# Splitting the mix of a soft mixture-of-experts layer into fp32r products of high and low parts

## The chip, the cores and the metric

The kernel runs on one core of a Trainium2 chip. The time is the device time of one execution in microseconds (us). Before the change it is 192.72 us, the median of three runs (192.67 to 193.3).

## The reference

One perceiver layer on x (128 rows of 256), all in fp32:

```python
x = x + cross_attention(layernorm(x), ctx)      # ctx: 12544 rows of 256
x = x + hyena(layernorm(x))                     # two long convolutions, gated
x = x + soft_moe(layernorm(x))

# soft_moe, E = 16 experts with 64 slots each, F = 512
x  = layernorm(x, norm_g, norm_b)
se = layernorm(slot_embeds, slot_g, slot_b) * scale
logits   = einsum('bnd,esd->bnes', x, se)
dispatch = softmax(logits, axis=1)
combine  = softmax(logits.reshape(b, n, E * S), axis=-1)
slots = einsum('bnd,bnes->besd', x, dispatch)
gate  = gelu(einsum('besd,edf->besf', slots, Wg) + bg)
up    = einsum('besd,edf->besf', slots, Wu) + bu
eout  = einsum('besf,efo->beso', gate * up, Wd) + bd
return einsum('bns,bso->bno', combine, eout)    # the mix
```

## The kernel before

The program is written by hand: each engine has its own list of instructions, in the order in which they run, and semaphores tie the lists together. Three stages follow one another. The attention (to 104 us of the span) goes over 98 tiles of 128 context rows in groups of four. It already works with split operands: a tile is kept as a high part, rounded to fp32r, and a low part, the remainder, and a product of two such operands is three fp32r matmuls (high by high, high by low, low by high). For the context rows POOL makes half of the high parts (L1001, a sum with a zero that is broadcast) and all low parts (L1006, a difference); PE weighs them at L457, L459 and L461. The hyena stage follows, to 124 us.

The last stage is the layer of experts, from 125 us on. Sixteen experts are taken as eight pairs p of 128 slots. For each pair PE computes gate and up (`hidden_of`, L663: per expert a 64-column weight tile and 512 moving columns, fp32), transposes the product of the two (`hidden_transpose`, L718), multiplies by the down weights into bank 4 (`down_of`, L676) and adds the pair's share of the output (`mix_of`, L726). DVE adds the bias to gate (L1276) and up (L1288), multiplies them into hid (L1297) and adds the down bias into eout (L1319), which has two buffers. ACT computes the gelu (L947), copies the transposed hid (L975) and issues the load of the bias rows for the pair three later (L977 to L980). There are three slots of bias rows, and DVE waits for a slot before the gate of its pair (L1270). SP has issued all weight loads by 153.2 us. In this stage POOL has no work.

The order on PE is the loop at L738. In turn p it issues gate of pair p, the transposes of pair p-1, a mix, up of pair p, and down of pair p-1. The mixes stand so: pairs 0 and 1 in turn 3, pair 2 in turn 4, pair 3 in turn 5, pair 4 in turn 6, none in turn 7. In turn 8, which has no gate and no up, pair 5 comes ahead of the last transposes, pair 6 behind them, and pair 7 after the last down, in two halves. A mix of the kernel before is two fp32 matmuls with combT[p] as weights and 128 columns of eout as the moving side, one into bank 1 and one into bank 5, accumulated over all eight pairs. In the profile each fp32 matmul is two records.

combT, the transposed combine weights, is written by ACT in turn 2 (`combine_copy`, L939) into the tile that held the transposed dispatch weights. The pieces of the tail: ACT and DVE copy half of the last transposed hid each (L972, L1307), DVE adds the bias to the two halves of the last eout (L1312), and after the last mixes DVE scales by rs and adds x2 (L1327). Two output DMAs follow.

Of the kernel before, what the change touches and what calls it, by code (L numbers as in the profile page):

```python
# [13 lines left out]
def perceiver_kernel(nc, x, ctx_in, xattn_W, proj_w, proj_b, filter_time, norm_g, norm_b,  # L14
                     scale, slot_embeds, Wg, Wu, Wd, biases, columns, tables, out):
    fp32 = mybir.dt.float32
    fp32r = mybir.dt.float32r
    ALU = mybir.AluOpType
# [3 lines left out]
    P = 128  # L22
    D = x.shape[2]
    DK = D // P
# [27 lines left out]
    with st:  # L52
        def sem(name):
            return st.enter_context(nc.semaphore(name))

        def sb(name, shape, dt=fp32, where=st):
            return where.enter_context(nc.sbuf_tensor(name, shape, dt))
# [3 lines left out]

        tab = sb("tab", [P, 5, P])
        ident, dft_c, dft_s, inv_c, inv_s = (tab[:, i, :] for i in range(5))
        x_sb = sb("x_sb", [P, D])
        x1 = sb("x1", [P, D])
        x2 = sb("x2", [P, D])
        xh = sb("xh", [P, D])
        xhT = sb("xhT", [P, DK, P])
        xn = sb("xn", [P, D])
        xnT = sb("xnT", [P, DK, P])  # L70
        stat6 = sb("stat6", [P, 6])
        mv = sb("mv", [P, 2])
        rstd = sb("rstd", [P, 1])
# [60 lines left out]
        ffn = ExitStack()  # L134
        late_gu = [sb(f"late_gu{i}", [P, 2, 2, DK, F], fp32, ffn) for i in range(EARLY, WSLOTS - 1)] + [last_gu]
        late_d = [sb(f"late_d{i}", [P, 2, FC, D], fp32, ffn) for i in range(EARLY, WSLOTS - 1)] + [last_d]
        dT = sb("dT", [P, PAIRS, P], fp32, ffn)
        combT = dT
        disp = sb("disp", [P, P], fp32, ffn)
        disp_hi = sb("disp_hi", [P, 4 * P], fp32r, ffn)  # L140
        disp_lo = sb("disp_lo", [P, 4 * P], fp32r, ffn)
        xn_hi = sb("xn_hi", [P, D], fp32r, ffn)
        xn_lo = sb("xn_lo", [P, D], fp32r, ffn)
        comb = sb("comb", [P, SLOTS], fp32, ffn)
        cmax = sb("cmax", [P, PAIRS], fp32, ffn)
        csum = sb("csum", [P, PAIRS], fp32, ffn)
        cinv = sb("cinv", [P, PAIRS], fp32, ffn)
# [58 lines left out]
        slots_ps, slots_rdy = sem("slots_ps"), sem("slots_rdy")  # L206
        rmax_rdy, cexp_rdy = sem("rmax_rdy"), sem("cexp_rdy")
        combT_ps, combT_rdy = sem("combT_ps"), sem("combT_rdy")
        gate_ps, up_ps, gate_rdy, up_rdy = sem("gate_ps"), sem("up_ps"), sem("gate_rdy"), sem("up_rdy")
        gelu_rdy, hid_rdy, hidT_ps, hidT_rdy = (sem("gelu_rdy"), sem("hid_rdy"), sem("hidT_ps"),  # L210
                                                sem("hidT_rdy"))
# [63 lines left out]
        def cols(h):  # L275
            return slice(h * P, (h + 1) * P)
# [90 lines left out]
        UP_BANK = (2, 0)  # L367
        SE_BANK = (6, 4, 2, 6)
        V_BANK, FREQ_BANK, CONV_BANK = (2, 0), (4, 1), (5, 3)
        MIX_BANK = (1, 5)  # L370

        LAST_T_BANK, LAST_DOWN_BANK = (3, 0), (4, 6)

# [2 lines left out]
        def _(pe):  # L376
# [347 lines left out]
                last.then_inc(hidT_ps, 1)  # L724

            def mix_of(p):  # L726
                pe.wait_ge(eout_rdy, p + 1)
                if p == 0:
                    pe.wait_ge(combT_rdy, 2)
                for h in range(2):  # L730
                    if p == PAIRS - 1:
                        pe.wait_ge(eout_rdy, p + 1 + h)
                    last = nc.tensor.matmul(bank[MIX_BANK[h]][:, 0:P], combT[:, p, :], eout[:, p % 2, cols(h)],  # L733
                                            start=(p == 0), stop=(p == PAIRS - 1))
                    if h == 1 or p == PAIRS - 1:
                        last.then_inc(mix_ps, 1)

            for p in range(PAIRS + 1):  # L738
                if p < PAIRS:
                    if p in (0, 1, 3):  # L740

                        pe.wait_ge(slots_rdy, {0: 2, 1: 4, 3: 6}[p])
                    if p >= 2:
                        pe.wait_ge(gate_rdy, p - 1)
                    hidden_of(p, 0, (6, 7)[p % 2], gate_ps)
                if p == 0:
                    logits(2)
                    first_logits_back()
                    transpose_dispatch(1)

                if p == PAIRS:
                    mix_of(PAIRS - 3)
                if p == PAIRS:
                    last_transpose()
                elif p >= 2:
                    hidden_transpose(p - 1)
                if p == 3:
                    mix_of(0)
                if p >= 3 and p != PAIRS - 1:
                    mix_of(p - 2)  # L760
                if p < PAIRS:
                    if p >= 2:
                        pe.wait_ge(up_rdy, p - 1)
                    hidden_of(p, 1, UP_BANK[p % 2], up_ps)
                if p == 0:
                    gather(1)
                    transpose_logits(2)
                    hidden_transpose(0)
                if p == 2:
                    transpose_dispatch(2)  # L770
                    combine_transpose(0)
                if p == PAIRS:
                    last_down()
                elif p >= 1:
                    down_of(p - 1)
                if p == 2:
                    gather(2)
                    combine_transpose(1)
# [204 lines left out]
        @block.gpsimd  # L983
        def _(pool):
            nc.gpsimd.memset(zero[:, :], 0.0).then_inc(const_set, 1)
            nc.gpsimd.memset(neg_half[:, :], -0.5).then_inc(const_set, 1)
            nc.gpsimd.memset(ones_sq[:, :], 1.0).then_inc(sq_set, 1)
            pool.wait_ge(const_set, 2)

            def power(n, dst, src, width):  # L990
                pool.wait_ge(var_rdy, n + 1)
                nc.gpsimd.tensor_tensor(dst, src, neg_half[:, 0:width], ALU.pow).then_inc(rstd_rdy, 1)

            power(0, rstd[:, 0:1], mv[:, 1:2], 1)

            def split_ctx(loop, g, slot, nt):

                pool.wait_ge(ld_raw[slot], raw_count(loop, g))
                if loop is not None or g >= RING:
                    pool.wait_ge(pv_ps, times(loop, g - RING + 1))  # L1000
                nc.gpsimd.tensor_tensor(c_hi[:, slot, 0:nt // 2, 0:D], raw[:, slot, 0:nt // 2, :],  # L1001
                                        zero[:, 0:1].unsqueeze(2).broadcast_to([P, nt // 2, D]), ALU.add
                                        ).then_inc(chi_rdy, 1)
                pool.wait_ge(chi_rdy, times(loop, g + 1))
                pool.wait_ge(chi2_rdy, times(loop, g + 1))
                nc.gpsimd.tensor_tensor(c_lo[:, slot, 0:nt, :], raw[:, slot, 0:nt, :],  # L1006
                                        c_hi[:, slot, 0:nt, 0:D].bitcast(fp32), ALU.subtract
                                        ).then_inc(clo_rdy, 1)

            for g in range(RING):  # L1010
                split_ctx(None, g, g, GT)
            with pool.Fori(0, LOOPS) as n:
                for u in range(RING):
                    split_ctx(n, RING + u, u, GT)
            split_ctx(None, LAST, LAST % RING, LAST_T)
            power(1, rstd[:, 0:1], mv[:, 1:2], 1)
            power(2, se_rstd[:, :], se_mv[:, :, 1], PAIRS)
            power(3, rstd[:, 0:1], mv[:, 1:2], 1)


        @block.vector
        def _(dve):
            count = [0]

            def link(ins):

                count[0] += 1
                ins.then_inc(dve_n, 1)
                dve.wait_ge(dve_n, count[0])
# [238 lines left out]
            for p in range(PAIRS + 1):  # L1268
# [36 lines left out]
                if p == PAIRS:  # L1305
                    dve.wait_ge(hidT_ps, p + 1)
                    nc.vector.tensor_copy(hidT[:, 2:4, :].rearrange("p c s -> p (c s)"),  # L1307
                                          bank[LAST_T_BANK[1]][:, 0:2 * P]).then_inc(hidT2_rdy, 1)
                    dve.wait_ge(mix_ps, p - 2)
                    for h in range(2):  # L1310
                        dve.wait_ge(down_ps, p + h)
                        nc.vector.tensor_tensor(eout[:, (p - 1) % 2, cols(h)], bank[LAST_DOWN_BANK[h]][:, 0:P],  # L1312
                                                bias[:, (p - 1) % BSLOTS, 2 * F + h * P:2 * F + (h + 1) * P], ALU.add
                                                ).then_inc(eout_rdy, 1)
                elif p >= 1:
                    dve.wait_ge(down_ps, p)
                    if p >= 3:
                        dve.wait_ge(mix_ps, p - 2)
                    nc.vector.tensor_tensor(eout[:, (p - 1) % 2, :], bank[4][:, 0:D],  # L1319
                                            bias[:, (p - 1) % BSLOTS, 2 * F:2 * F + D], ALU.add  # L1320
                                            ).then_inc(eout_rdy, 1)
# [2 lines left out]

            for h in range(2):
                dve.wait_ge(mix_ps, PAIRS + h)
                nc.vector.scalar_tensor_tensor(out=x1[:, cols(h)], in0=bank[MIX_BANK[h]][:, 0:P], scalar=rs[:, 3:4],  # L1327
                                               in1=x2[:, cols(h)], op0=ALU.mult, op1=ALU.add).then_inc(res_rdy, 1)


# [39 lines left out]
```

## Time and profile before

| | before |
|---|---|
| median of three runs | 192.72 us (192.67 to 193.3) |
| the profiled execution | 192.84 us, its span 190.8 us |
| PE matmul busy | 186.3 us, 98% of the span, 1268 instructions |
| DVE busy | 125.9 us, 66% |
| ACT busy | 108.9 us, 57% |
| POOL busy | 82.3 us, 43%, 61 instructions |
| DMA | 47.01 MB, mean 246 GB/s |

The profile comes from one execution, which took 192.84 us. Its span, from the first to the last recorded instruction, is 190.8 us; the rest lies around it. Times in the rows below are counted from the start of the span. A row of a timeline gives the start, the length of the merged group, the engine, the line of the kernel, the operation with what it writes and reads, and the count; in brackets stands how long the engine idled before and what released it. Matmuls overlap, so the price of one in a sequence is read from the distance between starts and not from its own length. PE is the matrix engine, PEld its weight loads, DVE the vector engine, ACT the scalar engine, POOL GpSimd.

### The profile page before, as it was taken

What the parts mean: (1) busy time and instruction counts of PE and PEld (TensorE: products, weight loads), DVE (VectorE), ACT (ScalarE), POOL (GpSimd) and SP (SyncE); (2) the same over time, 40 slices, a digit from 0 to 9 for tenths busy, and PEclk for the clock granted to TensorE, in tenths of its full rate; (3) what the DMA queues carried; (4) which work ended last, traced back from release to release, by engine and by line L of the source; (5) the groups of instructions that cost most, each with busy time, mean ns of one, the idle gap of its engine ahead of it and who ended that gap; (6) DMA issues with size and microseconds to landing.
All of it is one profiled execution on the core that took longest, in us unless ns stands there. A gap on an engine that the chain in (4) does not pass through costs nothing.

```text
span 190.8 us, 3969 instructions
## 1 busy us (share of the span) xinstructions
PE 186.3 (98%) x1268; PEld 146.1 (77%) x1268; DVE 125.9 (66%) x273; ACT 108.9 (57%) x226; POOL 82.3 (43%) x61
## 2 busy tenths in 40 slices
PE   8999999999999999999999999999999999999994
PEld 6888999999999999999989989974544555454463
DVE  3576997797777778777777888753673513524542
ACT  3568688777767767767776542967358521112210
POOL 2687979688778678877768013100000000000000
PEclk9999999999999999999999999999999999999999
DMA  5999958747784773974594399999999999983200
GB/s 182 328 345 379 344 170 277 252 137 228 250 267 155 278 252 113 353 233 155 126 239 103 111 365 383 354 373 368 381 365 380 283 363 284 275 208 93 77 0 28
DMA packets 25051, 47.01 MB, mean 246 GB/s; under 512 B 1616, under 2 KB 12112, under 8 KB 25040
## 3 DMA queue, kind: packets, MB, share of 16 engines
q1 hardware_dynamic: 23808, 43.52, 69.0%
q10 hardware_dynamic: 1232, 3.35, 7.1%
q8 instruction: 6, 0.10, 0.2%
q14 instruction: 5, 0.04, 0.1%
HBM read 46.73 MB, written 0.13 MB: 246 GB/s over the span
## 4 chain that ended last, share of the span: by engine, by line
PE 96%; ACT 1%; DVE 1%; issue 1%; POOL 0%; DVEq 0%; ACTq 0%; POOLq 0%
PE bank L671 15%; PE bank L416 11%; PE bank L685 6%; PE bank L457 6%; PE bank L461 6%; PE bank L459 6%; PE bank L429 6%; PE bank L433 6%; PE bank L431 6%; PE bank L442 6%; PE bank L733 2%; PE bank L723 2%; PE bank L385 2%; PE bank L558 2%; PE bank L576 2%; PE bank L549 1%
## 5 line engine op out<-in xcount | busy, mean ns | idle before, releaser
L1006 POOL TENSOR_TENSOR c_lo<-raw,c_hi 128x1024 fp32r<-128x1024 f32 (+1 forms) x25 | 54.0, 2159 | 19.9 <-ACT c_hi L802 19.9
L1084 DVE TENSOR_TENSOR cT_lo<-bank,cT_hi 128x512 fp32r<-128x512 f32 (+1 forms) x50 | 31.7, 675 | 9.7 <-ACT cT_hi L829 8.6
L829 ACT ACTIVATE cT_hi<-bank 128x512 fp32r<-128x512 f32 (+1 forms) x48 | 25.6, 585 | 9.8 <-PE bank L416 9.7
L457 PE MATMUL bank<-c_hi,pT_hi 128*128 128x258 f32 x98 | 29.9, 305 | 0.0
L461 PE MATMUL bank<-c_hi,pT_lo 128*128 128x258 f32 x98 | 27.7, 282 | 0.0
L459 PE MATMUL bank<-c_lo,pT_hi 128*128 128x256 f32 x98 | 27.5, 281 | 0.0
L1001 POOL TENSOR_TENSOR c_hi<-raw,zero 128x512 fp32r<-128x512 f32 (+1 forms) x25 | 25.6, 1025 | 1.7 <-DMA raw<-in_ctx_dram 1.7
L416 PE MATMUL bank<-tab,raw 128*128 128x128 f32 x196 | 25.6, 273 | 0.2 <-DVE cT_lo L1084 0.2
L836 ACT ACTIVATE pT_hi<-bank 128x512 fp32r<-128x512 f32 (+1 forms) x25 | 14.8, 590 | 14.4 <-PE bank L442 14.4
L416 PEld LDWEIGHTS bank<-tab,raw 128*128 128x128 f32 x196 | 22.1, 141 | 0.8 <-issue 0.3
L429 PE MATMUL bank<-cT_hi,q_hi 128*128 128x512 f32 (+1 forms) x50 | 21.5, 430 | 0.0
L1102 DVE TENSOR_TENSOR pT_lo<-bank,pT_hi 128x512 fp32r<-128x512 f32 (+1 forms) x25 | 17.0, 679 | 5.2 <-ACT pT_hi L836 5.0
L1096 DVE TENSOR_SCALAR_CACHE_REDUCE nsc<-bank,s,negm 128x512 f32<-128x512 f32 (+1 forms) x25 | 19.8, 794 | 0.8 <-PE bank L433 0.7
L844 ACT ACTIVATE prob<-nsc,negm 128x512 f32<-128x512 f32 (+1 forms) x25 | 17.7, 710 | 3.3 <-DVE nsc L1096 2.9
L433 PE MATMUL bank<-cT_hi,q_lo 128*128 128x512 f32 (+1 forms) x50 | 19.5, 390 | 0.0
L431 PE MATMUL bank<-cT_lo,q_hi 128*128 128x512 f32 (+1 forms) x50 | 19.3, 386 | 0.0
L459 PEld LDWEIGHTS bank<-c_lo,pT_hi 128*128 128x128 f32 x98 | 18.7, 190 | 0.0
L461 PEld LDWEIGHTS bank<-c_hi,pT_lo 128*128 128x128 f32 x98 | 18.5, 189 | 0.0
L457 PEld LDWEIGHTS bank<-c_hi,pT_hi 128*128 128x128 f32 x98 | 18.5, 189 | 0.0
L802 ACT ACTIVATE c_hi<-raw 128x512 fp32r<-128x512 f32 (+1 forms) x25 | 15.6, 625 | 0.0
L671 PE MATMUL bank<-early_gu,slots_or_se 128*64 128x512 f32 x64 | 15.2, 600 | 0.0
L1112 DVE SCALAR_TENSOR_TENSOR O<-O,alpha,bank 128x258 f32<-128x258 f32 x25 | 12.1, 482 | 4.3 <-PE bank L461 2.9
(178 smaller groups left out, 291.7 us busy)
## 6 DMA issues: line engine op xcount, KB each, us to landing
raw<-in_ctx_dram SPq DMA_DIRECT2D x24, 512.0 KB, 3.7
bias<-biases_dram ACTq DMA_DIRECT2D x10, 320.0 KB, 7.0
late_gu<-in_L_ffn_Wg_dram SPq DMA_DIRECT2D x3, 1024.0 KB, 10.4
late_gu<-in_L_ffn_Wu_dram SPq DMA_DIRECT2D x3, 1024.0 KB, 11.3
late_d<-in_L_ffn_Wd_dram SPq DMA_DIRECT2D x3, 1024.0 KB, 14.1
early_gu<-in_L_ffn_Wg_dram SPq DMA_DIRECT2D x4, 512.0 KB, 5.1
early_gu<-in_L_ffn_Wu_dram SPq DMA_DIRECT2D x4, 512.0 KB, 4.8
early_d<-in_L_ffn_Wd_dram SPq DMA_DIRECT2D x4, 512.0 KB, 5.2
```

Of the source, the lines that this page charges most:

```text
L416: last = nc.tensor.transpose(bank[h][:, t * P:(t + 1) * P], raw[:, slot, t, h * P:(h + 1) * P], ident)
L429: nc.tensor.matmul(bank[2 + r][:, 0:n], q_hi[:, h, :], cT_hi[:, r, h, 0:n], start=(h == 0), stop=False)
L431: nc.tensor.matmul(bank[2 + r][:, 0:n], q_hi[:, h, :], cT_lo[:, r, h, 0:n], start=False, stop=False)
L433: last = nc.tensor.matmul(bank[2 + r][:, 0:n], q_lo[:, h, :], cT_hi[:, r, h, 0:n], start=False, stop=(h == DK - 1))
L457: nc.tensor.matmul(bank[6 + r][:, 0:D + 2], ph, c_hi[:, slot, t, :], start=(t == 0), stop=False)
L459: nc.tensor.matmul(bank[6 + r][:, 0:D], ph, c_lo[:, slot, t, :], start=False, stop=False)
L461: last = nc.tensor.matmul(bank[6 + r][:, 0:D + 2], pl, c_hi[:, slot, t, :], start=False, stop=(t == nt - 1))
L671: last = nc.tensor.matmul(bank[b][a * SL:(a + 1) * SL, :], slotsT[:, k, p * P + a * SL:p * P + (a + 1) * SL], w_gu(s, which, a, a + 1)[:, ...
L829: nc.scalar.activation(cT_hi[:, g % 2, h, 0:n], bank[h][:, 0:n], ACT.Copy).then_inc(cThi_rdy, 1)
L1001: nc.gpsimd.tensor_tensor(c_hi[:, slot, 0:nt // 2, 0:D], raw[:, slot, 0:nt // 2, :], zero[:, 0:1].unsqueeze(2).broadcast_to([P, nt // 2, D ...
L1006: nc.gpsimd.tensor_tensor(c_lo[:, slot, 0:nt, :], raw[:, slot, 0:nt, :], c_hi[:, slot, 0:nt, 0:D].bitcast(fp32), ALU.subtract).then_inc(cl ...
L1084: nc.vector.tensor_tensor(cT_lo[:, g % 2, h, 0:n], bank[h][:, 0:n], cT_hi[:, g % 2, h, 0:n].bitcast(fp32), ALU.subtract).then_inc(cTlo_rdy, 1)
```

## The change

The mixes of pairs 0 to 5 become three fp32r matmuls each, 256 columns wide, into bank 1: high by high, high by low, low by high. POOL makes the parts. `split_eout(p)` waits for eout of the pair and, from pair 2 on, for the mix of pair p-2, which used the same buffer; it makes the high part and then the low part. `split_combine` does the same for the combine weights, first of four pairs (512 elements), then of two (256). The low part of the combine weights lies where combT lies, the high part where comb lies. The parts of eout lie over x_sb and its neighbours.

The mixes of pairs 6 and 7 stay fp32 and go into banks 5 and 2 as a sum of their own. DVE adds the first sum to x2 in the tail, between its copy of hidT and the last eout.

The order of the mixes on PE: none in turn 3, pairs 0 and 1 in turn 4, 2 and 3 in turn 5, 4 in turn 6. Turn 8 keeps pair 5 ahead of the last transposes and pair 6 behind them. DVE's additions into eout wait from pair 2 on for the split of the pair that had the buffer, not for its mix.

```diff
--- before.py
+++ after.py
@@ -61,13 +61,18 @@
 
         tab = sb("tab", [P, 5, P])
         ident, dft_c, dft_s, inv_c, inv_s = (tab[:, i, :] for i in range(5))
-        x_sb = sb("x_sb", [P, D])
         x1 = sb("x1", [P, D])
         x2 = sb("x2", [P, D])
-        xh = sb("xh", [P, D])
-        xhT = sb("xhT", [P, DK, P])
-        xn = sb("xn", [P, D])
         xnT = sb("xnT", [P, DK, P])
+
+        early = ExitStack()
+        x_sb = sb("x_sb", [P, D], fp32, early)
+        xh = sb("xh", [P, D], fp32, early)
+        xhT = sb("xhT", [P, DK, P], fp32, early)
+        xn = sb("xn", [P, D], fp32, early)
+        early.close()
+        eout_hi = sb("eout_hi", [P, 2, D], fp32r)
+        eout_lo = sb("eout_lo", [P, 2, D], fp32r)
         stat6 = sb("stat6", [P, 6])
         mv = sb("mv", [P, 2])
         rstd = sb("rstd", [P, 1])
@@ -134,14 +139,22 @@
         ffn = ExitStack()
         late_gu = [sb(f"late_gu{i}", [P, 2, 2, DK, F], fp32, ffn) for i in range(EARLY, WSLOTS - 1)] + [last_gu]
         late_d = [sb(f"late_d{i}", [P, 2, FC, D], fp32, ffn) for i in range(EARLY, WSLOTS - 1)] + [last_d]
-        dT = sb("dT", [P, PAIRS, P], fp32, ffn)
+
+
+        whole = ExitStack()
+        dT = sb("dT", [P, PAIRS, P], fp32, whole)
         combT = dT
+        comb = sb("comb", [P, SLOTS], fp32, whole)
+        whole.close()
+        combT_lo = sb("combT_lo", [P, PAIRS - 2, P], fp32r, ffn)
+        sb("last_combT", [P, 2 * P], fp32, ffn)
+        combT_hi = sb("combT_hi", [P, PAIRS - 2, P], fp32r, ffn)
+        sb("last_comb", [P, 2 * P], fp32, ffn)
         disp = sb("disp", [P, P], fp32, ffn)
         disp_hi = sb("disp_hi", [P, 4 * P], fp32r, ffn)
         disp_lo = sb("disp_lo", [P, 4 * P], fp32r, ffn)
         xn_hi = sb("xn_hi", [P, D], fp32r, ffn)
         xn_lo = sb("xn_lo", [P, D], fp32r, ffn)
-        comb = sb("comb", [P, SLOTS], fp32, ffn)
         cmax = sb("cmax", [P, PAIRS], fp32, ffn)
         csum = sb("csum", [P, PAIRS], fp32, ffn)
         cinv = sb("cinv", [P, PAIRS], fp32, ffn)
@@ -206,6 +219,7 @@
         slots_ps, slots_rdy = sem("slots_ps"), sem("slots_rdy")
         rmax_rdy, cexp_rdy = sem("rmax_rdy"), sem("cexp_rdy")
         combT_ps, combT_rdy = sem("combT_ps"), sem("combT_rdy")
+        chi_done, csplit_rdy, ehi_done, esplit_rdy = sem("chi_done"), sem("csplit_rdy"), sem("ehi_done"), sem("esplit_rdy")
         gate_ps, up_ps, gate_rdy, up_rdy = sem("gate_ps"), sem("up_ps"), sem("gate_rdy"), sem("up_rdy")
         gelu_rdy, hid_rdy, hidT_ps, hidT_rdy = (sem("gelu_rdy"), sem("hid_rdy"), sem("hidT_ps"),
                                                 sem("hidT_rdy"))
@@ -367,7 +381,7 @@
         UP_BANK = (2, 0)
         SE_BANK = (6, 4, 2, 6)
         V_BANK, FREQ_BANK, CONV_BANK = (2, 0), (4, 1), (5, 3)
-        MIX_BANK = (1, 5)
+        MIX_BANK, LAST_MIX_BANK = 1, (5, 2)
 
         LAST_T_BANK, LAST_DOWN_BANK = (3, 0), (4, 6)
 
@@ -724,16 +738,24 @@
                 last.then_inc(hidT_ps, 1)
 
             def mix_of(p):
-                pe.wait_ge(eout_rdy, p + 1)
-                if p == 0:
+                if p < PAIRS - 2:
+
+                    pe.wait_ge(esplit_rdy, p + 1)
+                    pe.wait_ge(csplit_rdy, p // 4 + 1)
+                    to = bank[MIX_BANK][:, 0:D]
+                    nc.tensor.matmul(to, combT_hi[:, p, :], eout_hi[:, p % 2, :], start=(p == 0), stop=False)
+                    nc.tensor.matmul(to, combT_hi[:, p, :], eout_lo[:, p % 2, :], start=False, stop=False)
+                    nc.tensor.matmul(to, combT_lo[:, p, :], eout_hi[:, p % 2, :], start=False, stop=(p == PAIRS - 3)
+                                     ).then_inc(mix_ps, 1)
+                else:
+
                     pe.wait_ge(combT_rdy, 2)
-                for h in range(2):
-                    if p == PAIRS - 1:
-                        pe.wait_ge(eout_rdy, p + 1 + h)
-                    last = nc.tensor.matmul(bank[MIX_BANK[h]][:, 0:P], combT[:, p, :], eout[:, p % 2, cols(h)],
-                                            start=(p == 0), stop=(p == PAIRS - 1))
-                    if h == 1 or p == PAIRS - 1:
-                        last.then_inc(mix_ps, 1)
+                    for h in range(2):
+                        pe.wait_ge(eout_rdy, p + 1 + (h if p == PAIRS - 1 else 0))
+                        last = nc.tensor.matmul(bank[LAST_MIX_BANK[h]][:, 0:P], combT[:, p, :], eout[:, p % 2, cols(h)],
+                                                start=(p == PAIRS - 2), stop=(p == PAIRS - 1))
+                        if h == 1 or p == PAIRS - 1:
+                            last.then_inc(mix_ps, 1)
 
             for p in range(PAIRS + 1):
                 if p < PAIRS:
@@ -754,10 +776,8 @@
                     last_transpose()
                 elif p >= 2:
                     hidden_transpose(p - 1)
-                if p == 3:
-                    mix_of(0)
-                if p >= 3 and p != PAIRS - 1:
-                    mix_of(p - 2)
+                for m in {4: (0, 1), 5: (2, 3), 6: (4,), PAIRS: (PAIRS - 2,)}.get(p, ()):
+                    mix_of(m)
                 if p < PAIRS:
                     if p >= 2:
                         pe.wait_ge(up_rdy, p - 1)
@@ -1016,6 +1036,35 @@
             power(1, rstd[:, 0:1], mv[:, 1:2], 1)
             power(2, se_rstd[:, :], se_mv[:, :, 1], PAIRS)
             power(3, rstd[:, 0:1], mv[:, 1:2], 1)
+
+            def split_eout(p):
+
+                pool.wait_ge(eout_rdy, p + 1)
+                if p >= 2:
+                    pool.wait_ge(mix_ps, p - 1)
+                nc.gpsimd.tensor_tensor(eout_hi[:, p % 2, :], eout[:, p % 2, :], zero[:, 0:1].broadcast_to([P, D]),
+                                        ALU.add).then_inc(ehi_done, 1)
+                pool.wait_ge(ehi_done, p + 1)
+                nc.gpsimd.tensor_tensor(eout_lo[:, p % 2, :], eout[:, p % 2, :], eout_hi[:, p % 2, :].bitcast(fp32),
+                                        ALU.subtract).then_inc(esplit_rdy, 1)
+
+            def split_combine(half):
+
+                tiles = slice(4 * half, 4 * half + 4 - 2 * half)
+                pool.wait_ge(combT_rdy, 2)
+                nc.gpsimd.tensor_tensor(combT_hi[:, tiles, :], combT[:, tiles, :],
+                                        zero[:, 0:1].unsqueeze(2).broadcast_to([P, 4 - 2 * half, P]), ALU.add
+                                        ).then_inc(chi_done, 1)
+                pool.wait_ge(chi_done, half + 1)
+                nc.gpsimd.tensor_tensor(combT_lo[:, tiles, :], combT[:, tiles, :],
+                                        combT_hi[:, tiles, :].bitcast(fp32), ALU.subtract).then_inc(csplit_rdy, 1)
+
+            split_eout(0)
+            split_combine(0)
+            split_eout(1)
+            split_combine(1)
+            for p in range(2, PAIRS - 2):
+                split_eout(p)
 
 
         @block.vector
@@ -1306,7 +1355,11 @@
                     dve.wait_ge(hidT_ps, p + 1)
                     nc.vector.tensor_copy(hidT[:, 2:4, :].rearrange("p c s -> p (c s)"),
                                           bank[LAST_T_BANK[1]][:, 0:2 * P]).then_inc(hidT2_rdy, 1)
-                    dve.wait_ge(mix_ps, p - 2)
+
+                    dve.wait_ge(mix_ps, PAIRS - 2)
+                    link(nc.vector.scalar_tensor_tensor(out=x2[:, :], in0=bank[MIX_BANK][:, 0:D], scalar=rs[:, 3:4],
+                                                        in1=x2[:, :], op0=ALU.mult, op1=ALU.add))
+                    dve.wait_ge(esplit_rdy, p - 2)
                     for h in range(2):
                         dve.wait_ge(down_ps, p + h)
                         nc.vector.tensor_tensor(eout[:, (p - 1) % 2, cols(h)], bank[LAST_DOWN_BANK[h]][:, 0:P],
@@ -1315,7 +1368,7 @@
                 elif p >= 1:
                     dve.wait_ge(down_ps, p)
                     if p >= 3:
-                        dve.wait_ge(mix_ps, p - 2)
+                        dve.wait_ge(esplit_rdy, p - 2)
                     nc.vector.tensor_tensor(eout[:, (p - 1) % 2, :], bank[4][:, 0:D],
                                             bias[:, (p - 1) % BSLOTS, 2 * F:2 * F + D], ALU.add
                                             ).then_inc(eout_rdy, 1)
@@ -1324,7 +1377,7 @@
 
             for h in range(2):
                 dve.wait_ge(mix_ps, PAIRS + h)
-                nc.vector.scalar_tensor_tensor(out=x1[:, cols(h)], in0=bank[MIX_BANK[h]][:, 0:P], scalar=rs[:, 3:4],
+                nc.vector.scalar_tensor_tensor(out=x1[:, cols(h)], in0=bank[LAST_MIX_BANK[h]][:, 0:P], scalar=rs[:, 3:4],
                                                in1=x2[:, cols(h)], op0=ALU.mult, op1=ALU.add).then_inc(res_rdy, 1)
```

## Rows read from the trace of the kernel before

**Rows 1.** The page: busy time, and the granted clock in 40 slices.

```profile
PE 186.3 (98%) x1268; PEld 146.1 (77%) x1268; DVE 125.9 (66%) x273; ACT 108.9 (57%) x226; POOL 82.3 (43%) x61
...
PEclk9999999999999999999999999999999999999999
```

**Rows 2.** Timeline of PE, expert stage, turns 3 to 7.

```profile
154.01 0.66 PE L723 MATMUL bank<-tab,hid 128*128 128x128 f32 x4
...
161.83 1.94 PE L671 MATMUL bank<-late_gu,slots_or_se 128*64 128x512 f32 x8
...
167.14 0.66 PE L723 MATMUL bank<-tab,hid 128*128 128x128 f32 x4
167.64 0.61 PE L733 MATMUL bank<-eout,dT 128*128 128x128 f32 x4
168.18 1.94 PE L671 MATMUL bank<-last_gu,slots_or_se 128*64 128x512 f32 x8
169.94 1.90 PE L685 MATMUL bank<-late_d,hidT 128*64 128x256 f32 x16
...
173.98 0.61 PE L733 MATMUL bank<-eout,dT 128*128 128x128 f32 x4
...
179.83 0.66 PE L723 MATMUL bank<-tab,hid 128*128 128x128 f32 x4
180.42 1.94 PE L671 MATMUL bank<-early_gu,slots_or_se 128*64 128x512 f32 x8
```

**Rows 3.** Timeline of DVE in turn 4.

```profile
164.18 0.18 DVE L1241 RECIPROCAL cinv<-csum 128x4 f32<-128x4 f32 x1 [4.55 <-DMA bias<-biases_dram]
...
165.89 0.69 DVE L1297 TENSOR_TENSOR hid<-gate,up 128x512 f32<-128x512 f32 x1
166.50 0.42 DVE L1319 TENSOR_TENSOR eout<-bank,bias 128x256 f32<-128x256 f32 x1
```

**Rows 4.** Chain of waits in the attention (start, us, what): twelve matmuls between.

```profile
63.36 0.12 PE bank L457
...
64.84 0.87 PE bank L416 x8
```

**Rows 5.** Groups by line and form, POOL (busy us, mean ns, idle before).

```profile
L1006 POOL TENSOR_TENSOR c_lo<-raw,c_hi 128x1024 fp32r<-128x1024 f32 x24 | 52.8, 2200 | 19.4 <-ACT c_hi L802 19.4
...
L1006 POOL TENSOR_TENSOR c_lo<-raw,c_hi 128x512 fp32r<-128x512 f32 x1 | 1.2, 1187 | 0.5 <-ACT c_hi L802 0.5
L1001 POOL TENSOR_TENSOR c_hi<-raw,zero 128x256 fp32r<-128x256 f32 x1 | 0.6, 622 | 0.0
```

**Rows 6.** Timeline, handoffs from DVE to POOL and back.

```profile
123.11 0.15 DVE L1216 TENSOR_SCALAR mv<-mv 128x1 f32<-128x1 f32 x1
...
123.35 0.55 POOL L992 TENSOR_TENSOR rstd<-mv,neg_half 128x1 f32<-128x1 f32 x1 [7.42 <-DVE mv L1216]
...
123.93 0.60 DVE L1220 TENSOR_SCALAR xh<-x,mv,rstd 128x128 f32<-128x128 f32 x2 [0.66 <-POOL rstd L992]
```

**Rows 7.** Timeline of ACT: second combine copy, bias loads of pair 4.

```profile
151.99 0.59 ACT L942 ACTIVATE dT<-bank 128x512 f32<-128x512 f32 x1
...
154.71 1.13 ACTq L232 DMA_DIRECT2D bias<-biases_dram  x2
```

**Rows 8.** Timeline of PE, turn 2: fp32r matmuls after a wait.

```profile
149.77 0.50 PE L638 MATMUL bank<-disp_hi,xn_hi 128*128 128x512 f32 x1
150.11 0.40 PE L639 MATMUL bank<-disp_lo,xn_hi 128*128 128x512 f32 x1
150.35 0.40 PE L640 MATMUL bank<-disp_hi,xn_lo 128*128 128x512 f32 x1
```

**Rows 9.** Timeline of DVE, end of turn 5.

```profile
172.73 0.42 DVE L1319 TENSOR_TENSOR eout<-bank,bias 128x256 f32<-128x256 f32 x1
```

**Rows 10.** Timeline of DVE, turn 8.

```profile
186.75 0.29 DVE L1312 TENSOR_TENSOR eout<-bank,bias 128x128 f32<-128x128 f32 x1 [1.12 <-PE bank L702]
```

**Rows 11.** All instructions that touch the bias rows: how long loads take.

```profile
DMA to landing us min/median/max: 3.9/6.9/8.9
```

## The prediction

> **What bounds the kernel now.** The page comes first [rows 1]: PE is busy for 186.3 of 190.8 us, and its granted clock shows the full level, 2.4 GHz, in all 40 slices. POOL has no instruction after 123.9 us, the whole expert stage. So what shortens PE's queue shortens the kernel, as long as nobody makes PE wait. The timeline of PE in the expert stage comes second [rows 2]: each pair runs gate, transposes, mix, up, down with no idle time written beside a row. The change touches the mix.
>
> The third question is how early each operand of PE is there, because a bound engine tolerates lateness only up to its slack. Pair 4's turn on DVE is the place to look [rows 3]: DVE idled 4.55 us for the bias rows and so made gate, up, hid and, last, eout of pair 3, from 166.50 to 166.92. PE transposed hid at 167.14 and mixed at 167.64 [rows 2]. Hid, ready at 166.58, had 0.56 us to spare; eout of pair 3, had mix 3 stood there, 0.72.
>
> **The price of a mix.** From the start of the transposes to the start of the up matmuls PE takes 0.59 us without a mix (179.83 to 180.42) and 1.04 with one (167.14 to 168.18) [rows 2]. One fp32 mix is 0.45 us. The new mix is three fp32r matmuls with a 256-wide moving side and a weight load each. The attention has just these: twelve of them, from 63.36 to the chain's next piece at 64.84, are 1.48 us, 0.123 each [rows 4]. A new mix is 0.37 and saves 0.08, six times: **0.48 us**, a ceiling.
>
> The Trainium skill speaks on this too: FP8 and Floating Point Precision (TensorE Precision Notes) counts true fp32 as four passes, high and low parts crossed. Three passes for four would save an estimated quarter of 0.45, 0.11, and the end would be 0.18 us earlier than I forecast; the rows say 0.08, and the sum goes by them.
>
> **The price of a split.** The high part is a POOL copy of 256 elements: 0.622 us, seen once in this very shape. The low part is seen at 1.187 (512 elements) and 2.200 (1024): 256 elements extrapolate to 0.68 [rows 5]. POOL starts 0.09 us after the DVE instruction that releases it, and DVE 0.03 after POOL [rows 6]. I take 0.08 into POOL and between its own two, 0.06 into PE. From the end of eout to the first mix matmul: 0.08+0.62+0.08+0.68+0.06 = **1.52 us** in place of some 0.06. Bounds: the slope alone (0.51 each, nothing fixed) gives 1.24, two instructions as long as the 512-element one (1.19 each) 2.6. I take 1.52, which rests on rows of this size.
>
> [...]
>
> **Pair by pair** (turn p is named by its pair; clock of the trace; minus is earlier).
> Pair 3: mixes 0 and 1 leave it, -0.90; its up starts at 154.01+0.59 = 154.60.
> Pair 4: mixes 0 and 1 stand there, 0.74, in place of mix 2, 0.45: its up at 161.22 instead of 161.83, -0.61. Their operands are ready. The second combine copy ends at 152.58 [rows 7]; POOL then splits 512 elements (at most 0.08+1.19+0.08+1.19), eout 1 and 256 more (1.46 each), to 158.0; mix 0 starts at 160.4. Without that cover each us of lateness would be one of PE. Eout 2 is split when mix 0 is over, 161.0 to 162.5, under 4 us of other work.
> Pair 5: PE is ready to transpose at 167.14-0.61 = 166.53. But hid of pair 4 doesn't move: it hangs on the bias DMA that the ACT queue issued at 154.71, right after the hid copy of pair 2, ahead of every mix that changes [rows 7]. Hid reaches PE at 166.64: first small wait, 0.11. Mix 2 goes from 167.14 to 167.51. Mix 3 stands behind it and needs the split of eout 3: 166.92+1.52 = **168.44. PE waits 0.93 us**, with the up matmuls of pair 5 queued behind. The first load after a wait isn't hidden: an fp32r matmul after one starts 0.34 before its successor, the successor 0.24 before the next [rows 8]; +0.11. Then 0.37 for the mix and 0.09 before the up matmuls (0.59 less 0.50 for the transposes): up at 169.01, against 168.18 before, **+0.83**.
> Pair 6: the down matmuls ended at 171.84, now at 172.67; DVE stands at 173.15 with eout 4 by the old bias chain [rows 9] and by the new PE at 173.14. Its split is there at 174.67. PE comes to mix 4 at 173.98+0.83 = 174.81: 0.14 us to spare. Mix 4 saves 0.08: +0.75. The bias rows of pair 5 are issued up to 0.9 us earlier, which can only help.
> Pair 7 has no mix. Ahead of the last transposes mix 5 saves 0.08, with its split over since about 180: **+0.67**. The mixes of pairs 6 and 7 stay fp32, in other banks, at no price.
> The tail on DVE: a new multiply-add of 128x256 comes after the hidT copy. DVE idled 1.12 us there for the down matmuls, until 186.75 [rows 10]; a 256-wide DVE instruction from PSUM is 0.42 [rows 3], with its own wait some 0.5: hidden, and 0.5 if that cover were gone.
> The waits of DVE's eouts move from mixes to splits that are over at least 1 us earlier. No DMA is added or moved. That the parts lie over comb and dT costs no wait beyond the combine copies.
>
> **The sum.** The profiled execution is 192.84 us for a span of 190.8, 0.12 above the median of 192.72. 192.84+0.67 = 193.51; against the median **193.4 us**, 0.35% slower. A measurement of this kernel can tell about 0.3%, 0.58 us, from no change.
>
> **Rivals.**
> Not slower, the stall stays away. What decides is when the bias rows of pair 4 land: each 0.1 us earlier takes 0.1 off the wait at mix 3, and 0.93 earlier it is gone (POOL's lower bound alone takes off 0.28). Pair 5's up then starts at 166.64+0.59+0.74 = 167.97, -0.21, and mixes 4 and 5 make it -0.37: 192.35 us; without the hid wait -0.48, 192.24. For it: landing takes 3.9 to 8.9 us in this trace [rows 11]. Against: issue and traffic beside it are the same in both kernels. Chance 0.2.
> Two stalls. With a split 0.3 us longer than 1.52 (POOL's handoff to itself is in no row) mix 3 is 0.3 later, eout 4 hangs on PE and ends at 173.44, its split at 175.26, and PE is there at 175.11 and waits 0.15, with 0.11 for the load: 0.67+0.3+0.26 = +1.23, 193.95 us. It decides from 0.14 us of excess on. At the 512-element bound it would be over +2; no row of this size is near. Chance 0.25.
> The forecast, one stall of 0.6 to 1.2 us: chance 0.55.
> A gain of over 0.3% is more than the ceiling: 0.04, the new matmuls being faster than any row, taken from the first rival.
>
> **How the numbers follow.** Within 0.3% lie the rest of the first rival, 0.16, and the lower part of the forecast, whose centre is 0.1 us over that bound, 0.24: 0.40. Slower by more: 0.31+0.25 = 0.56. The range goes from the no-stall case, 192.3, to two stalls with a split 0.35 over, 194.1.
>
> **What would show it.** PE waits for POOL's eout_lo once, in pair 5's turn, for about 0.9 us; the 256-wide splits take 0.62 and 0.68; pair 3's up starts 0.59 after its transposes; new matmuls start 0.12 apart. The forecast is wrong if mix 3 starts within 0.2 us of mix 2's end, if POOL needs under 1.2 us from eout's end to its last write, or if the new matmuls are over 0.15 apart, in which case the mixes gain nothing at all.

## The result, and the profile after

The changed kernel takes 194.29 us, the median of 18 runs (193.09 to 195.06). The kernel before takes 193.16 in 18 runs (192.62 to 194.05), so the three runs shown ahead of the prediction, 192.72, lay 0.4 us low. The ratio is 1.0058 with a 95% interval of 1.0042 to 1.0074: **the change costs 1.1 us**. I had forecast 0.7, and my range ended 0.2 us short of the measured median.

Busy times and the granted clock after, from the page:

```profile
span 192.4 us, 3984 instructions
...
PE 186.7 (97%) x1262; PEld 145.8 (76%) x1262; DVE 126.5 (66%) x274; ACT 108.9 (57%) x226; POOL 94.0 (49%) x77
...
PEclk9999999999999999999999999999999999999999
```

The clock is still at its upper level [rows 1]. The span has grown by 1.6 us; the time of these two executions has grown by 1.4 (194.24 against 192.84), since the part of it that lies outside the span is shorter in the changed kernel. I come back to that behind the experiments. Busy time hides what happened: the stalls have to be looked for in the rows. Of those 1.6 us, 0.45 came before anything was changed (the gate of pair 3 starts at 152.59 here, at 152.14 before, and a second profile of the kernel before has it at 153.03, so this much is chance). When I write "on the stage's clock" below, times are shifted so that this gate starts at 152.14.

The timeline of PE after, from the transposes of turn 3 to turn 7, answers to [rows 2]:

```profile
154.46 0.66 PE L737 MATMUL bank<-tab,hid 128*128 128x128 f32 x4
155.04 1.94 PE L685 MATMUL bank<-late_gu,slots_or_se 128*64 128x512 f32 x8
...
160.35 0.66 PE L737 MATMUL bank<-tab,hid 128*128 128x128 f32 x4
...
161.65 1.94 PE L685 MATMUL bank<-late_gu,slots_or_se 128*64 128x512 f32 x8
...
166.96 0.65 PE L737 MATMUL bank<-tab,hid 128*128 128x128 f32 x4
...
167.69 0.28 PE L748 MATMUL bank<-eout_hi,combT_lo 128*128 128x256 f32 x1
168.21 0.39 PE L746 MATMUL bank<-eout_hi,combT_hi 128*128 128x256 f32 x1 [0.24 <-POOL eout_lo L1048]
168.43 0.28 PE L747 MATMUL bank<-eout_lo,combT_hi 128*128 128x256 f32 x1
...
168.76 1.94 PE L685 MATMUL bank<-last_gu,slots_or_se 128*64 128x512 f32 x8
...
174.07 0.66 PE L737 MATMUL bank<-tab,hid 128*128 128x128 f32 x4
175.72 0.39 PE L746 MATMUL bank<-eout_hi,combT_hi 128*128 128x256 f32 x1 [0.99 <-POOL eout_lo L1048]
...
176.27 1.94 PE L685 MATMUL bank<-early_gu,slots_or_se 128*64 128x512 f32 x8
```

Turn 3 has no mix any more: 0.58 from the transposes to the up matmuls. Turn 4 has two: 1.30, so one new mix is 0.36, where the old one was 0.45 [rows 2]. Then come two waits with POOL as the releaser. Mix 3 (168.21) should have followed mix 2 at 167.81. Mix 4 (175.72) comes 1.65 after its transposes started, where an unstalled one comes 0.41 after them (the first mix of turn 4 is at 160.76). So the wait in turn 5 costs 0.4, and 0.1 more because the first matmul behind it starts 0.22 and not 0.12 ahead of its successor; the wait in turn 6 costs 1.2.

What DVE and POOL did ahead of the second wait, timelines of the two engines:

```profile
171.64 0.75 DVE L1325 SCALAR_TENSOR_TENSOR gate<-bank,cinv,bias 128x512 f32<-128x512 f32 x1 [4.98 <-DMA bias<-biases_dram]
172.30 0.74 DVE L1337 SCALAR_TENSOR_TENSOR up<-bank,cinv,bias 128x512 f32<-128x512 f32 x1
173.14 0.69 DVE L1346 TENSOR_TENSOR hid<-gate,up 128x512 f32<-128x512 f32 x1
173.75 0.42 DVE L1372 TENSOR_TENSOR eout<-bank,bias 128x256 f32<-128x256 f32 x1
```

```profile
174.25 0.61 POOL L1045 TENSOR_TENSOR eout_hi<-eout,zero 128x256 fp32r<-128x256 f32 x1 [6.09 <-DVE eout L1372]
174.94 0.73 POOL L1048 TENSOR_TENSOR eout_lo<-eout,eout_hi 128x256 fp32r<-128x256 f32 x1
```

Read it backwards. Mix 4 starts 0.05 after POOL's low part, that 0.08 after the high part, that 0.08 after eout; eout is the last of four DVE instructions in a row; the first of them waited 4.98 us for the bias rows of pair 5. In the kernel before DVE did the same four, from 170.62 on, and nobody noticed, since eout was wanted at 173.98 [rows 2, 9]. On the stage's clock the rows landed 0.57 us later now, and the split put 1.5 us between eout and the mix. In a second profile of the changed kernel (after_again, below) they landed 0.85 us later than before.

### The profile page after: what moved, and what is told of

It reads as the page before. It is cut to its first block, busy times and chain, and to the rows that moved or that the text cites. A ratio compares the mean times of both kernels' runs of the same rounds, so it can differ in the third digit from the quotient of the medians.

```text
span 192.4 us, 3984 instructions
## 1 busy us (share of the span) xinstructions
PE 186.7 (97%) x1262; PEld 145.8 (76%) x1262; DVE 126.5 (66%) x274; ACT 108.9 (57%) x226; POOL 94.0 (49%) x77
## 4 chain that ended last, share of the span: by engine, by line
PE 94%; POOL 1%; ACT 1%; DVE 1%; issue 1%; DVEq 0%; POOLq 0%; ACTq 0%
PE bank L685 15%; PE bank L430 11%; PE bank L699 6%; PE bank L471 6%; PE bank L475 6%; PE bank L473 6%; PE bank L443 6%; PE bank L447 6%; PE bank L445 6%; PE bank L456 6%; PE bank L399 2%; PE bank L572 2%; PE bank L590 2%; PE bank L737 1%; PE bank L405 1%; PE bank L563 1%
## 5 line engine op out<-in xcount | busy, mean ns | idle before, releaser
L1045 POOL TENSOR_TENSOR eout_hi<-eout,zero 128x256 fp32r<-128x256 f32 x6 | 3.7, 613 | 37.4 <-DVE eout L1372 34.1
```

## The experiments

Theory A: PE waits for POOL's parts because eout of pairs 3 and 4 is made late, behind the bias loads, and the new mixes gain as computed. Theory B: the new mixes, the moved mixes or POOL's work beside DVE cost by themselves. Ratios are to the kernel before, with their 95% intervals; each kernel was timed in 11 or 12 runs; where I give such a ratio in us, it is of 193.1. The kernel before was also profiled once more, in one run of 193.73 us (before_again), to see how far the landing of the bias rows moves by chance: those of pair 5 were there at 171.63, which is 170.74 on the stage's clock, against 170.62 in the first profile.

**No late bias rows.** In both kernels ACT no longer loads the rows of pairs 3 to 7:

```diff
-                if p >= 1 and p - 1 + BSLOTS < PAIRS:
-                    act.wait_ge(eout_rdy, p)
-                    load_bias(act, p - 1 + BSLOTS)
...
-                    dve.wait_ge(ld_bias[p % BSLOTS], 32 * (p // BSLOTS + 1))
+                    dve.wait_ge(ld_bias[p % BSLOTS], 32)
```

> The kernel before, with the bias rows of pairs 3 to 7 not loaded (those pairs use the rows of pairs 0 to 2, so this part of the sum is another one). DVE's waits for bias rows in turns 4 and 5 are gone. Both theories: in the kernel before nobody on PE waited for DVE there, so 0 to -0.2 us against before (193.1).

> The changed kernel, with the bias rows of pairs 3 to 7 not loaded. Theory A (the loss is PE waiting for POOL's parts because eout of pairs 3 and 4 is made late, behind the bias loads; the mixes themselves gain 0.08 us each): both waits of PE for eout_lo are gone and the time is 0.3 to 0.5 us below nobias_before. Theory B (the new mixes, the moved mixes or POOL's work beside DVE cost by themselves): it stays 0.5 us or more above nobias_before.

Measured: nobias_before 193.09 us, 0.9997 (0.9981 to 1.0014); nobias_after 192.60 us, 0.9953 (0.9933 to 0.9973). The changed kernel is now faster than the unchanged one under the same condition, by 0.49 us from median to median and by 0.85 by the two ratios. PE waits for POOL nowhere. Turn 6 of nobias_after on PE, the place of the former wait:

```profile
174.04 0.65 PE L737 MATMUL bank<-tab,hid 128*128 128x128 f32 x4
174.45 0.36 PE L746 MATMUL bank<-eout_hi,combT_hi 128*128 128x256 f32 x1
...
174.98 1.51 PE L685 MATMUL bank<-early_gu,slots_or_se 128*64 128x512 f32 x6
```

0.94 from the transposes to the up matmuls, 0.36 more than without a mix. Theory B is out: the arithmetic gains what it should and the loss needs the late rows.

**The order alone.** All mixes fp32, in the new order, with two more buffers for eout (the edits for these are left out here):

```diff
...
-                if p == 3:
-                    mix_of(0)
-                if p >= 3 and p != PAIRS - 1:
-                    mix_of(p - 2)
+                for m in {4: (0, 1), 5: (2, 3), 6: (4,), PAIRS: (PAIRS - 2,)}.get(p, ()):
+                    mix_of(m)
...
```

> The kernel before with the order of mixes of the changed one (0 and 1 in turn 4, 2 and 3 in turn 5, 4 in turn 6), all mixes fp32, with four buffers for eout and no splits. Theory A: eout of pair 3 is ready 0.7 us before its mix, so 0.0 (+-0.2) us against before. Theory B in its form that the moved mixes cost: +0.5 us or more.

Measured: 193.64 us, 1.0012 (0.9990 to 1.0033). By the ratio that is +0.2 us (-0.2 to +0.6), the upper edge of what was expected; the medians are 0.5 apart. The profile shows that the order isn't quite free: turn 4 starts 0.9 us earlier on PE, DVE doesn't, and PE waited 0.28 us for hid of pair 4.

```profile
167.48 0.66 PE L730 MATMUL bank<-tab,hid 128*128 128x128 f32 x4 [0.28 <-DVE hid L1302]
```

**Mixes 3 and 4 one turn later.**

```diff
-                for m in {4: (0, 1), 5: (2, 3), 6: (4,), PAIRS: (PAIRS - 2,)}.get(p, ()):
+                for m in {4: (0, 1), 5: (2,), 6: (3,), 7: (4,), PAIRS: (PAIRS - 2,)}.get(p, ()):
```

> The changed kernel with mixes 3 and 4 one turn later on PE: 0 and 1 in turn 4, 2 in turn 5, 3 in turn 6, 4 in turn 7. POOL has a whole turn, 6 us, for each split. Theory A: no wait for eout_lo, -0.3 to -0.5 us against before, 192.6 to 192.8. Theory B: nothing of what costs is taken away, +0.5 to +1.1 us against before.

Measured: 192.99 us, 0.9985 (0.9968 to 1.0002). The 1.1 us of loss are gone, and no wait for POOL is left. But 192.6 to 192.8 was expected, so the mending falls short by 0.2 to 0.4 us. It isn't the full gain, since hid of pair 5 hangs on the same bias rows (landed at 171.71) and PE needs it in turn 6 wherever the mixes stand:

```profile
173.96 0.66 PE L737 MATMUL bank<-tab,hid 128*128 128x128 f32 x4 [0.57 <-DVE hid L1346]
```

**The bias rows issued earlier.** ACT issues the rows of pairs 4 to 7 ahead of its wait for the transposes, not behind its hid copy. No load is left out:

```diff
+                if 2 <= p and p - 1 + BSLOTS < PAIRS:
+                    act.wait_ge(eout_rdy, p)
+                    load_bias(act, p - 1 + BSLOTS)
                 act.wait_ge(hidT_ps, p + 1)
...
-                if p >= 1 and p - 1 + BSLOTS < PAIRS:
+                if p == 1:
```

> The kernel before, with the bias rows of pairs 4 to 7 issued by ACT ahead of its hid copy instead of behind it (eout, which frees the slot, is there 2 to 4 us earlier than that copy). All loads stay. Theory A: PE was never waiting for these rows in the kernel before, or by 0.3 us in some executions: 0 to -0.2 us against before.

> The changed kernel with the same earlier issue of the bias rows. Theory A (lateness of eout behind the bias loads): the rows of pair 4 land before 163 us and those of pair 5 before 170.5, both waits for eout_lo go and the time is -0.3 to -0.5 us against before. Rival (the loads are served no sooner, since the weights stand ahead of them in the DMA engines): landing times as now, +0.6 us or more against before.

> Both mendings: mixes 3 and 4 one turn later and the bias rows issued earlier. Theory A: like eb_after, -0.4 to -0.5 us against before, and no wait of PE for hid either; the 0.2 us that the version with the later mixes alone lacks of that was PE waiting for hid of pair 5, so it is regained.

Measured: eb_before 193.23 us, 0.9999 (0.9982 to 1.0016). **eb_after 192.42 us, 0.9961 (0.9945 to 0.9978), which beats both kernels.** eb_later 192.58 us, 0.9963 (0.9942 to 0.9984), so what the later mixes alone had lacked is regained. Both gained about 0.7 us, more than the 0.3 to 0.5 that were expected. DVE in eb_after, turns 4 to 6:

```profile
161.40 0.18 DVE L1293 RECIPROCAL cinv<-csum 128x4 f32<-128x4 f32 x1 [2.32 <-DMA bias<-biases_dram]
...
165.26 0.42 DVE L1375 TENSOR_TENSOR eout<-bank,bias 128x256 f32<-128x256 f32 x1 [0.25 <-PE bank L699]
168.88 0.75 DVE L1328 SCALAR_TENSOR_TENSOR gate<-bank,cinv,bias 128x512 f32<-128x512 f32 x1 [3.19 <-DMA bias<-biases_dram]
...
171.87 0.42 DVE L1375 TENSOR_TENSOR eout<-bank,bias 128x256 f32<-128x256 f32 x1 [0.25 <-PE bank L699]
```

DVE still waits for both loads, but the releaser in front of eout is now PE's down matmuls and no longer the chain behind the bias rows. From then on the 1.5 us of the split fit. The same edit is worth nothing in the kernel before, where nothing was waiting for eout.

**Which of the two waits counts.** One mix moved at a time (edits of the same line: mix 3 to turn 6, or mix 4 to turn 7), and, for the length of the split, ACT making the high part in place of POOL (ACT's waits for eout and for the mix that used the buffer are left out here):

```diff
-                nc.gpsimd.tensor_tensor(eout_hi[:, p % 2, :], ... ALU.add).then_inc(ehi_done, 1)
...
+                    nc.scalar.activation(eout_hi[:, (p - 1) % 2, :], eout[:, (p - 1) % 2, :], ACT.Copy
+                                         ).then_inc(ehi_done, 1)
```

> The changed kernel with mix 3 alone one turn later, beside mix 4 in turn 6. Theory A, sharpened: the wait that sets the end is the one at mix 4, because eout of pair 4 hangs on the landing of pair 5's bias rows and not on PE, so what mix 3 waits in turn 5 is only taken out of the wait at mix 4. The time stays that of the changed kernel (+1.1 us against before, +-0.3). My prediction's version (the wait at mix 3 is the loss, 0.9 us): +0.2 us or less against before.

> The changed kernel with mix 4 alone one turn later, in turn 7. Theory A, sharpened: the wait of 1 us at mix 4 goes, the wait at mix 3 of 0.5 to 1 us now counts, with some wait for hid of pair 5 instead: +0.1 to +0.5 us against before, clearly under the changed kernel. My prediction's version: no change from the changed kernel, +0.9 us or more.

> The changed kernel with the high part of eout copied by ACT (about 0.4 us) and only the low part by POOL: the way from eout to the mix is 0.2 to 0.25 us shorter. Theory A: PE still waits at mixes 3 and 4, and since the waits overlap the gain counts once: 0.2 to 0.3 us below the changed kernel. If both waits added up it would be 0.4 to 0.6.

> The changed kernel once more, beside the three above on the same chip, with a second profile. Theory A: 194.2 +-0.3, PE waits for eout_lo at mix 3 or mix 4 or both, together as much as the rows of pair 5 are late; pair 5's rows land after 171 us on the clock of the stage. If they land before 170.5 here, the wait at mix 4 is under 0.3 us and the span is shorter by as much.

Measured: after_again 194.17 us, 1.0043 (1.0021 to 1.0064), the loss again. mix3_later 193.90 us, 1.0013 (0.9989 to 1.0038); mix4_later 193.56 us, 1.0012 (0.9987 to 1.0038); act_hi 194.43 us, 1.0058 (1.0025 to 1.0091). The expectation for after_again holds: pair 5's rows landed at 171.47 on the stage's clock. That for mix3_later (+0.8 us or more) is missed by the ratio, +0.3 us (-0.2 to +0.7), while the medians, 193.90 against 193.11, are 0.8 apart; so this run doesn't exclude the prediction's version, +0.2 or less. mix4_later, +0.2 us (-0.3 to +0.7), lies where it was expected and excludes the prediction's version, +0.9 or more; its interval and that of after_again overlap, so it isn't shown to be faster than the changed kernel. act_hi shows no gain, against 0.2 to 0.3 us expected, but its way from eout to the mix was only 0.17 shorter (1.39 us, from 167.16 to 168.55), and its runs spread over more than 2 us, so 0.2 can't be seen in them. The profiles say why one wait alone doesn't carry it. PE's long waits in turns 5 and 6, in mix3_later, mix4_later and act_hi:

```profile
175.65 0.39 PE L746 MATMUL bank<-eout_hi,combT_hi 128*128 128x256 f32 x1 [0.82 <-POOL eout_lo L1048]
```

```profile
169.77 0.39 PE L746 MATMUL bank<-eout_hi,combT_hi 128*128 128x256 f32 x1 [0.82 <-POOL eout_lo L1048]
```

```profile
168.55 0.38 PE L746 MATMUL bank<-eout_hi,combT_hi 128*128 128x256 f32 x1 [0.66 <-POOL eout_lo L1052]
```

These are executions of two sorts. From the row of ACT's issue to the DVE row that had waited:

| profile | rows of pair 4 | rows of pair 5 |
|---|---|---|
| before, before_again | 9.5, 9.4 us | 9.1, 9.2 us |
| after, after_again, later, mix3_later | 8.8, 8.8, 8.7, 8.9 | 10.6, 10.9, 10.5, 10.5 |
| order_only, mix4_later, act_hi | 9.9, 9.9, 9.9 | 9.5, 9.7, 9.1 |

Where pair 4's rows are late, PE waits at hid and mix 3; where pair 5's are late, at mix 4, and whatever mix 3 had waited is then taken out of that wait. One mix moved mends one sort of execution. I read the middling ratios of mix3_later and mix4_later so; with one profile for each kernel that is an inference, not a count. Two things speak for it: eleven of mix3_later's twelve runs fall into two groups, four at 192.80 to 193.10 us and seven at 193.71 to 194.43, and the executions profiled of mix3_later and mix4_later, 194.17 and 194.53 us, lie in the upper part of their runs. Both profiles of the changed kernel itself are of the sort with pair 5's rows late.

**The sum of it.** From the gate of pair 3 to the last mix, on PE, in the kernel before, the changed kernel and nobias_after:

```profile
152.14 1.94 PE L671 MATMUL bank<-late_gu,slots_or_se 128*64 128x512 f32 x8 [0.25 <-ACT slots_or_se L927]
...
187.44 0.95 PE L733 MATMUL bank<-eout,dT 128*128 128x128 f32 x4
```

```profile
152.59 1.94 PE L685 MATMUL bank<-late_gu,slots_or_se 128*64 128x512 f32 x8 [0.25 <-ACT slots_or_se L947]
...
189.10 0.95 PE L755 MATMUL bank<-eout,dT 128*128 128x128 f32 x4
```

```profile
153.06 1.94 PE L685 MATMUL bank<-late_gu,slots_or_se 128*64 128x512 f32 x8 [0.25 <-ACT slots_or_se L947]
...
187.81 0.95 PE L755 MATMUL bank<-eout,dT 128*128 128x128 f32 x4
```

| kernel | this stretch | time outside the span, all runs |
|---|---|---|
| before, nobias_before, eb_before | 35.30 us each | 2.0 to 2.1 us |
| order_only | 35.64 | 2.0 to 2.1 |
| nobias_after, eb_after, eb_later | 34.75 each | 1.7 to 1.8 |
| later | 35.37 | 1.7 to 1.8 |
| after, after_again | 36.51, 36.79 | 1.7 to 1.8 |

So the six new mixes gain 0.55 us in the stretch wherever nothing waits, and the late rows turn that into a loss of 1.2 to 1.5. The second column is a term that no sum of mine had: each kernel with the new mixes spends some 0.27 us less outside the span than each kernel without them. What shortens it is in no trace, so the cause stays open. The two columns together give -0.8 us for eb_after, as measured against eb_before (192.42 against 193.23), and +0.9 to +1.2 for the changed kernel, measured +1.1.

## Why the prediction was right and wrong

The prediction was wrong by its range, and the step that failed is in pair 6: "The bias rows of pair 5 are issued up to 0.9 us earlier, which can only help." They were issued 0.9 earlier on the stage's clock (161.05 less 0.45, against 161.50) and landed 0.57 later, in the second profile 0.85. The stretch of the table above then came out at +1.21 and +1.49 against my +0.67, which is 0.54 and 0.82 too much: the lateness of the rows, almost to the digit. At mix 4 itself I had 0.14 us to spare and lost 1.2, for two reasons: its parts came 0.55 later than I had them, and PE came 0.8 earlier, since mix 3 had held it up less. The unforeseen 0.27 us outside the span took back a part of this. The general mistake was to treat the landing of both loads as fixed by the kernel before, while the core's DMA engines were fully busy (a share of 1.0 or more from 152 to 167 us in both kernels). Counted from the issue of pair 4's rows, pair 5's landed after 15.9 and 16.0 us in the kernel before, where they were issued 6.8 us behind those, and after 15.4 to 16.8 in the executions with the new order, where they were issued 5.9 behind. In the other sort of execution it is pair 4's rows that fail the prediction: in order_only, mix4_later and act_hi they landed 0.4 to 0.5 later on the stage's clock than the 164.18 on which hid of pair 4 and eout 3 were reckoned, and pair 5's then 0.1 to 0.5 earlier. In mix4_later up of pair 5 started at +1.31 against my +0.83. No profile caught the changed kernel itself in this sort.

Point by point. The price of a new mix was right: 0.36 against my 0.37. Beside the old 0.45 that saves 0.09, between the rows' 0.08 and the 0.11 estimated from what the Trainium skill's FP8 and Floating Point Precision (TensorE Precision Notes) says, four passes for true fp32 against the three of the split. The six together are 0.55 us in the traces without late rows, where I had 0.48 as the ceiling. The 0.49 between the medians of the nobias pair agrees with the ceiling by luck: its two ratios say 0.85, and 0.55 and the 0.27 outside the span make 0.8. The split was right in kind and nearly in size: from eout's end at 166.65 to the mix at 168.21 it took 1.56 us (0.61 and 0.73 of work) against 1.52. The low part is longer than the 0.68 I extrapolated. The Trainium skill's GPSIMD Engine Reference (section 3.1) gives about 2.6 cycles for each element of a two-input operation, at its 1.2 GHz an estimated 2.2 ns. The trace agrees: from the low part of 256 elements (0.73) to that of 512 (1.27, the combine weights) it is 2.1 ns an element. For the first load behind the wait I added 0.11 and it cost 0.10.

The wait at mix 3 was there: 0.4 us in this execution with pair 4's rows landing 0.7 earlier on the stage's clock than I took them, and 0.8 in mix4_later. But in the two profiles of the changed kernel it wasn't the one that set the end. I had foretold one wait for POOL; there were two. That the forecast isn't further off, although mix 3 waited 0.4 us and not 0.9, is luck: by my own reckoning mix 4's parts came only 0.14 ahead of PE, so the second wait stepped in for the first. The rival "two stalls" gave 193.95 at a chance of 0.25, and its +1.23 is close to the measured +1.1; its cause was wrong (a longer split), and the true one, later rows, was left out. The rival "not slower", had the rows come early, is what eb_after makes true: its 192.42 is 0.7 us under the kernel before. That 192.35 was forecast for it is luck in the number: the rival had -0.37 (-0.48 without the hid wait) on a base that lay 0.4 low. The tail was hidden as said: the new multiply-add took 0.47 and DVE still idled 0.76 us after it.

The starting point was off as well: the sum was made on a median of three runs that lay 0.4 us under the median of eighteen. Without that, the same forecast of +0.67 would have stood at 193.8 with its upper end at 194.5.

## What to carry to other kernels

When work is put between a producer and a bound engine, ask for the slack of the producer at its latest, not at its end in one trace: here eout hung on a DMA that had been late by 4 us all along at no cost, and 1.5 us of splitting made it count. Time from issue to landing in a busy queue isn't a constant, so an earlier issue is a gain only if the trace of that version shows an earlier landing. And a cheaper operation for the bound engine is worth only what its schedule lets through: the same change was worth -0.7 us or +1.1 us, by where one group of loads was issued. Last, compare the time outside the span too; here it moved by a quarter of the effect.

## What was not expected of the hardware

DVE's product hid in turn 3 took 0.99 us in place of 0.69 while POOL was writing a low part. The timelines of POOL and DVE in the changed kernel:

```profile
157.52 0.73 POOL L1059 TENSOR_TENSOR combT_lo<-dT,combT_hi 128x256 fp32r<-128x256 f32 x1
```

```profile
157.81 0.99 DVE L1346 TENSOR_TENSOR hid<-gate,up 128x512 f32<-128x512 f32 x1
```

It is the one place in the expert stage where a DVE instruction with both inputs in SBUF met a POOL instruction. In act_hi, where POOL's last part of this group was done at 156.94, ahead of hid at 157.19, hid took 0.69. The delay came 1.5 us ahead of the need for hid, so it cost nothing. The Trainium skill's SBUF — State Buffer (Who interferes with whom) says that a DVE instruction with two SBUF inputs contends with a GpSimd instruction that reads SBUF, for a port pair that one of them holds alone until it is done. A full hold until 158.25 and 0.69 after it would end at 158.94; the row ends at 158.80, so the trace agrees roughly. DVE's gate and up, with one input from PSUM, kept their 0.75 beside POOL's work (gate at 154.63, while POOL was busy from 154.22 to 155.49, and up at 157.03).

The landing times of the bias rows come in the patterns of the table above. What makes an execution take one or the other stays open; no run here tells it.
